# Flamingo-style gated cross attention with an RWKV feed-forward: a late weight load, its buffer, one split and the prologue put in another order

## What is computed

```python
x = x + tanh(g_xattn) * attention(layernorm(x), ctx, ctx, mask, q_w, q_b, k_w, k_b, v_w, v_b, o_w, o_b)
x = x + tanh(g_ffn) * ffn(layernorm(x), W_r, W_k, W_v, mu_r, mu_k)
# attention: Q, K, V = x@q_w.T+q_b, ctx@k_w.T+k_b, ctx@v_w.T+v_b, in 16 heads
#            softmax(Q K^T / sqrt(32), masked) V, then @ o_w.T + o_b
# ffn: x_prev is x moved down by one row; xr, xk = mu*x + (1-mu)*x_prev
#      sigmoid(xr @ W_r.T) * (relu(xk @ W_k.T)**2 @ W_v.T)
```

## Time and profile before

| | us |
|---|---|
| median of 3 runs | 1153.17 |
| lowest and highest | 1152.59, 1156.04 |
| the profiled execution | 1153.75 |
| its span, first to last instruction | 1151.9 |
| PE busy | 1118.8 (97%) |
| DVE busy | 888.4 (77%) |
| ACT busy | 686.3 (60%) |
| POOL busy | 367.6 (32%) |

### The profile page before, as it was taken

How to read it: one execution, slowest core, us unless ns; L and a number is a source line. 1 busy time by engine, 2 the same in 40 slices (tenths; PEclk the granted TensorE clock), 3 DMA queues, 4 the chain that set the end, 5 groups by cost and what they waited for, 6 DMA issues and landing times.

```text
span 1151.9 us, 21580 instructions
## 1 busy us (share of the span) xinstructions
PE 1118.8 (97%) x7216; PEld 895.2 (78%) x7216; DVE 888.4 (77%) x1964; ACT 686.3 (60%) x1527; POOL 367.6 (32%) x595
## 2 busy tenths in 40 slices
PE   5999999999999999999999999979999999999998
PEld 4677777777778778777877777757888888888886
DVE  7878877888788878887888788867677776776764
ACT  4767776777677767776777677753333323332232
POOL 0153153045045026116214302663442334323331
PEclk9999999999999999999999999989999999999999
DMA  8675575764775676567567557702311132111300
GB/s 284 199 199 146 166 212 153 193 193 132 199 203 131 192 207 171 139 196 214 149 168 211 141 144 229 222 12 74 99 55 56 55 95 71 55 55 62 103 20 37
DMA packets 95709, 162.48 MB, mean 141 GB/s; under 512 B 13296, under 2 KB 22640, under 8 KB 95472
## 3 DMA queue, kind: packets, MB, share of 16 engines
q1 hardware_dynamic: 84912, 143.37, 44.0%
q10 hardware_dynamic: 10688, 17.73, 5.4%
HBM read 109.91 MB, written 49.57 MB: 138 GB/s over the span
## 4 chain that ended last, share of the span: by engine, by line
PE 87%; DMA 3%; issue 2%; DVE 2%; POOL 1%; ACT 1%; SPq 0%; DVEq 0%; ACTq 0%; POOLq 0%
PE bank L550 26%; PE bank L624 18%; PE bank L586 14%; PE bank L615 10%; PE bank L636 9%; PE bank L594 8%; PE bank L749 1%; DMA w_raw<-wvvT 1%; ACT kact_hi L985 1%; PE bank L738 1%; DMA rden_dram<-ctx_sb 0%; DVE xh L1238 0%; POOL w2r_lo L1429 0%; DVE kact L1276 0%; DMA qk_dram<-q_hi 0%
## 5 line engine op out<-in xcount | busy, mean ns | idle before, releaser
L904 ACT ACTIVATE probs<-neg_s,negmax 128x512 f32<-128x512 f32 x512 | 368.1, 720 | 65.0 <-DVE negmax L1079 62.7
L1079 DVE CUSTOM_DVE_ANT_0 neg_s<-bank,mask_big 128x512 f32<-128x512 f32 x512 | 344.0, 679 | 9.7 <-DVE mask_big L1139 1.0
L624 PE MATMUL bank<-ident,probs 128*128 128x128 f32 x2048 | 307.6, 273 | 3.0 <-DVE pT L1085 2.9
L624 PEld LDWEIGHTS bank<-ident,probs 128*128 128x128 f32 x2048 | 248.1, 140 | 51.1 <-issue 6.1
L1085 DVE COPY pT<-bank 128x512 f32<-128x512 f32 x254 | 175.0, 689 | 110.2 <-PE bank L624 109.1
L615 PE MATMUL bank<-k_stack,q_stack 96*128 96x512 f32 x512 | 242.1, 473 | 0.2 <-DMA q_stack<-qk_dram 0.2
L911 ACT COPY pT<-bank 128x512 f32<-128x512 f32 x258 | 149.8, 580 | 127.6 <-PE bank L624 127.0
L636 PE MATMUL bank<-pT,v_sb 128*32 128x512 f32 x1024 | 116.5, 595 | 0.6
L983 ACT ACTIVATE relu<-bank 128x512 f32<-128x512 f32 x32 | 19.2, 599 | 145.3 <-PE bank L550 143.3
L615 PEld LDWEIGHTS bank<-k_stack,q_stack 96*128 96x128 f32 x512 | 97.3, 190 | 1.6 <-DMA q_stack<-qk_dram 0.5
L904 ACT ACTIVATION_READ_ACCUMULATOR probs<-neg_s,negmax 128x1 f32 x512 | 97.1, 190 | 0.0
(11 more groups left out here) (158 smaller groups left out, 2165.3 us busy)
## 6 DMA issues: line engine op xcount, KB each, us to landing
k_stack<-qk_dram SPq DMA_DIRECT2D x93, 256.0 KB, 5.4
q_stack<-qk_dram SPq DMA_DIRECT2D x93, 256.0 KB, 6.2
cT_raw<-ctxT SPq DMA_DIRECT2D x8, 1024.0 KB, 7.6
rden_bc<-rden_dram SPq DMA_DIRECT2D x128, 64.0 KB, 6.2
ctx_dram<-ctx_sb SPq DMA_DIRECT2D x32, 256.0 KB, 2.2
c_raw<-ctx_dram SPq DMA_DIRECT2D x16, 512.0 KB, 5.0
x_in<-x SPq DMA_DIRECT2D x16, 512.0 KB, 5.8
qk_dram<-k_hi SPq DMA_DIRECT2D x31, 256.0 KB, 2.7
```

The source lines that it names most:

```text
L624: mm = nc.tensor.transpose(pt_bank[i % 2][:, a * P:(a + 1) * P], probs[:, i % P_RING, a * P:(a + 1) * P], ident[:])
L904: nc.scalar.activation(probs[:, i % P_RING, :], neg_s[:, i % SM_RING, :], ACT.Exp, bias=negmax[:, k:k + 1], scale=-1.0, accum_out=den[:, g ...
L1079: nc.vector.tensor_tensor_reduce(neg_s[:, i % SM_RING, :], s_bank[tile_no(b, c, i) % S_BANKS][:], mask_big[:, q, :], 1.0, 3e38, ALU.add, A ...
```

## The change

The diff changes four things:

- **The fourth late weight** (wvv) is loaded into `w2_raw[0]`, the buffer of the first, as soon as that one is split, from SP's group 1 of the last batch (before: into `w2_raw[1]` after the second's split, from group 2). x1 moves over `w2_raw[1]`.
- **POOL's order at the passage:** the third split (wr) goes behind the inverse root and the second unit's context; the second bias goes ahead of the root.
- **Prologue:** `ident` is the first transfer after x; on PE the second keys go ahead of the first queries, and V0 takes the low part of the weight last; on ACT the first keys go ahead of the query weight's rounding; on DVE the mask goes ahead of Q0 and the scaling of the bias row (`gate_bias`) to step (1, 1); ACT starts the query copies after the high part of Q0.
- **Batch 1's x:** two of the four statistics go into the prologue, the others to steps (0, 9) and (0, 13); ACT's store, first two loads and spread go to steps (1, 0) to (1, 3), and the last load from (2, 0) to (1, 15).

```diff
@@ -78,8 +78,8 @@
     if nb == 1:
-        return {(0, 0, 0): ("xT", 0), (0, 0, 2): ("xT", 1), (0, 0, 12): ("store", 0), (0, 1, 0): ("spread", 0),
-                (0, 1, 14): ("xT", 2), (0, 2, 0): ("xT", 3)}
+        return {(0, 1, 0): ("store", 0), (0, 1, 1): ("xT", 0), (0, 1, 2): ("xT", 1), (0, 1, 3): ("spread", 0),
+                (0, 1, 14): ("xT", 2), (0, 1, 15): ("xT", 3)}
     return {(first, 3, 0): ("rows", 0), (first, 3, 2): ("rows", 1), (first, 3, 10): ("rows", 2),
@@ -87,7 +87,7 @@
-    return ((0, 0, 1), (0, 0, 3), (0, 0, 5), (0, 0, 7)) if nb == 1 else (
+    return (None, None, (0, 0, 9), (0, 0, 13)) if nb == 1 else (
         (nb - 2, 3, 7), (nb - 2, 3, 9), (nb - 1, 0, 3), (nb - 1, 0, 5))
@@ -206,7 +206,7 @@
-        x1 = [w2_raw[0][:, h * UM:(h + 1) * UM, :] for h in range(2)]
+        x1 = [w2_raw[1][:, h * UM:(h + 1) * UM, :] for h in range(2)]
         xh = sb(stage2, "xh", [P, UM, D])
@@ -351,9 +351,9 @@
                 load_x(t)
+            sp.dma_start(ident[:], ident_d).then_inc(ident_ld, 16)
             load_w(1, wk)
             load_ctx(0)
-            sp.dma_start(ident[:], ident_d).then_inc(ident_ld, 16)
             for t, a in ((bq_col, bq), (bk_col, bk)):
@@ -428,8 +428,8 @@
                 if n == 3:
-                    sp.wait_ge(w2_lo_done[1], 1)
-                sp.dma_start(w2_raw[n % 2][:], W2[n].rearrange("(a p) e -> p a e", p=P)).then_inc(w2_ld[n % 2], 16)
+                    sp.wait_ge(w2_lo_done[0], 1)
+                sp.dma_start(w2_raw[n % 3][:], W2[n].rearrange("(a p) e -> p a e", p=P)).then_inc(w2_ld[n % 3], 16)
@@ -481,8 +481,8 @@
                         load_turned(0, 1)
+                        load_w2(3)
                     if c == 2 and not more:
-                        load_w2(3)
                         load_w2r()
@@ -648,6 +648,18 @@
+            def first_values(keys):
+
+                for act_part, w in ((act_hi, w1_hi), (act_lo, w1_hi), (act_hi, w1_lo)):
+                    if w is w1_lo:
+                        pe.wait_ge(w_lo_done, 3)
+                    for a in range(CH):
+                        mm = nc.tensor.matmul(first_v_bank[:, keys * UNIT:(keys + 1) * UNIT],
+                                              act_part[1][:, a, keys * P:(keys + 1) * P], w[2][:, a, 0:UNIT],
+                                              start=act_part is act_hi and w is w1_hi and a == 0,
+                                              stop=w is w1_lo and a == CH - 1)
+                return mm
+
             def chunk_rounded(a):
@@ -663,26 +675,27 @@
+            product(1, 1, second_bank[1], w1_hi, act_hi, start=True)
+            product(1, 1, second_bank[1], w1_lo, act_hi)
+            product(1, 1, second_bank[1], w1_hi, act_lo, stop=True).then_inc(second_mm[1], 1)
+
             pe.wait_ge(w_hi_done, 2)
             pe.wait_ge(side_hi, hi_no(None, ("T", TT - 1)) + 1)
             product(0, 0, q_first, w1_hi, act_hi, start=True)
             pe.wait_ge(side_done, done(side_no(None, ("T", TT - 1))))
             product(0, 0, q_first, w1_hi, act_lo)
-            product(1, 1, second_bank[1], w1_hi, act_hi, start=True)
-            product(1, 1, second_bank[1], w1_lo, act_hi)
+            pe.wait_ge(side_done, done(side_no(None, ("K", 0))))
+            product(0, 1, second_bank[0], w1_hi, act_hi, start=True)
             pe.wait_ge(w_lo_done, 2)
             product(0, 0, q_first, w1_lo, act_hi, stop=True).then_inc(side_mm, 1)
-            product(1, 1, second_bank[1], w1_hi, act_lo, stop=True).then_inc(second_mm[1], 1)
-
-            pe.wait_ge(side_done, done(side_no(None, ("K", 0))))
-            product(0, 1, second_bank[0], w1_hi, act_hi, start=True)
             product(0, 1, second_bank[0], w1_hi, act_lo)
             product(0, 1, second_bank[0], w1_lo, act_hi, stop=True).then_inc(second_mm[0], 1)
-            pe.wait_ge(w_lo_done, 3)
-            side(None, "V", 0, 0, 2)
+
+            pe.wait_ge(w_hi_done, 3)
+            first_values(0)
             for i in range(AHEAD_S):
                 scores(0, 0, i)
-            side(None, "V", 0, 1, 2)
+            first_values(1).then_inc(side_mm, 1)
             scores(0, 0, AHEAD_S)
@@ -850,6 +863,8 @@
                 for band, source in enumerate((qk_hi, qk_hi, qk_lo)):
+                    if j == 0 and band == 2:
+                        act.wait_ge(side_done, done(side_no(None, ("Q", 0))))
                     act.dma_start(stack[0][0][HD * band:HD * (band + 1), j, :].bitcast(F32),
@@ -915,12 +930,12 @@
                     nc.scalar.mul(bq_neg[:], bq_col[:], -SCALE).then_inc(consts, 1)
+                if (kind, n) == ("Q", 0):
                     split_w(0)
-                if (kind, n) == ("Q", 0):
                     split_w(2)
                     act.wait_ge(consts, 1)
                 side(None, kind, n)
-            act.wait_ge(side_done, done(side_no(None, ("Q", 0))))
+            act.wait_ge(side_hi, hi_no(None, ("Q", 0)) + 1)
             for j in range(2):
@@ -1132,19 +1147,23 @@
             split_w(0)
+            dve.wait_ge(mask_ld, 16)
+            nc.vector.tensor_scalar(mask_big[:], mask_u8, MASKED, None, ALU.mult).then_inc(mask_done, 1)
             dve.wait_ge(consts, 1)
             side(None, "Q", 0)
             split_w(2)
-            dve.wait_ge(mask_ld, 16)
-            nc.vector.tensor_scalar(mask_big[:], mask_u8, MASKED, None, ALU.mult).then_inc(mask_done, 1)
+            for t in range(2):
+                row_stats(1, t)
             dve.wait_ge(mask_done, 1)
             mask_and_min(0, 0, 0)
             mask_and_min(0, 0, 1)
+            mask_and_min(0, 0, 2)
             dve.wait_ge(bv_ld, 16)
             side(None, "V", 0)
-            mask_and_min(0, 0, 2)
-            dve.wait_ge(consts, 2)
-            nc.vector.tensor_scalar(tgbo[:], tgbo[:], tg[:, 0:1], None, ALU.mult).then_inc(consts, 1)
+
+            def gate_bias():
+                dve.wait_ge(consts, 2)
+                nc.vector.tensor_scalar(tgbo[:], tgbo[:], tg[:, 0:1], None, ALU.mult).then_inc(consts, 1)
@@ -1160,6 +1179,8 @@
                         tile_step(b, c, i)
+                        if (b, c, i) == (0, 1, 1):
+                            gate_bias()
                         if i == TILES - 2:
@@ -1187,7 +1208,7 @@
                     if m == 0:
-                        dve.wait_ge(w2_lo_done[0], 1)
+                        dve.wait_ge(w2_lo_done[1], 1)
                         dve.wait_ge(xb_done, 1)
@@ -1416,11 +1437,11 @@
             def split_w2(n):
-                raw = w2r_raw if n == 2 else w2_raw[n % 2]
+                raw = w2r_raw if n == 2 else w2_raw[n % 3]
                 if n == 2:
                     pool.wait_ge(w2r_ld, 16)
                 else:
-                    pool.wait_ge(w2_ld[n % 2], 16 * (n // 2 + 1))
+                    pool.wait_ge(w2_ld[n % 3], 16 * (n // 3 + 1))
                 pool.wait_ge(side_mm, mm_no(B - 1, (("Q", 3), ("K", 3), ("V", 3), ("V", 3))[n]) + 1)
@@ -1450,10 +1471,10 @@
             split_w2(3)
-            split_w2(2)
+            first_bias(1)
             inverse_root2(0, 0)
             first_context(1)
-            first_bias(1)
+            split_w2(2)
             for b in range(B):
```

## The result

| | median (us) | lowest to highest | runs |
|---|---|---|---|
| before | 1154.86 | 1152.59 to 1156.04 | 7 |
| after | 1149.56 | 1146.58 to 1151.96 | 7 |

After over before is 0.9955, with a 95% interval of 0.9941 to 0.9969: 5.3 us or 0.45% faster. The forecast was 1144.2 with a range of 1141.5 to 1148.0. So the sign was right and the size was not: 9.0 us were forecast, and the median lies 1.6 above the range. Of the 5.4 us between 1149.56 and 1144.2, 1.7 lie in the kernel before, whose median over seven runs is 1154.86 and not the 1153.17 of the three that the forecast started from; the other 3.7 are the change. Note the spread too. The profiled execution of after, 1146.58 us for a span of 1144.7, is the fastest of its seven.

What follows compares the result with a forecast made beforehand. PE, busy 97% of the span, was taken as the bound, with stage 1 waits at the start and the passage. Passage 6.7 plus prologue 2.3 made 9.0 us off 1153.17, so 1144.2, range 1141.5 to 1148.0.

Steps and rivals of the forecast that it cites:

- The sum for the passage: Passage to stage 2: 6.95 us of DVE's wait and 1.3 of clock gained, 1.5 lost to POOL; 6.7 us net.
- The meeting of DVE and POOL: After the root, POOL's third split beside DVE's difference and mix: costs 1.5 us, bounds 0 and 3.
- Transfers around 719 to 743: Last batch: the fourth weight's megabyte ahead of SP's stores and stacks costs 0, with a loss of up to 3 us possible.
- The prologue up to group 1: Start of batch 0: first mask 0.8 us sooner, second keys' memory chain faster, q_stack landing at 47.7; 2.3 us gained.
- Batch 1's x costed at nothing: Later statistics, spread and loads of batch 1's x cost 0, with the steps of group 1 as cover.
- The clock: At the passage, a wait of 1.1 us keeps PE's clock, gaining 1.3 us; losing it would give 1145.5.
- The prologue gives nothing: Rival: q_stack lands where it did and only the passage's 6.7 us remains, 1146.5 us; chance 0.14.
- My list of what would be wrong: Signs against: PE waits for last-batch stacks or batch 0 group 2 cT/xT parts; POOL waits for x_in or fourth weight beyond 749.8.

Runs made afterwards that it cites:

- the run with the split ahead: The kernel with after's edits but the old x chain, with POOL's third split put ahead of the root again: 1148.29 us against its base's 1146.51.
- the passage alone: The kernel before with only the passage's edits (fourth weight's earlier load and buffer, POOL's order, x1): 1148.09 us, ratio 0.9943.
- the kernel with a mended chain: After with batch 1's statistics at steps 1 and 3, store at 12, two x loads at 13 and 14 of group 0, spread at (1, 0): 1144.95, again 1144.88 us.
- the old chain: After with batch 1's whole x chain (statistics, store, spread, loads) back at its steps of the kernel before: 1146.51 us, ratio 0.9933.
- the prologue alone: The kernel before with after's prologue edits and new x chain, without the passage's edits: 1154.95 us, ratio 1.0005.

## Why the prediction was right and wrong

**The sum for the passage: right.** 6.7 forecast, 6.6 measured alone. By its steps in the profile of after: the root starts at 749.75 (749.8 forecast), DVE's wait of 6.95 is gone, the clock at 763 to 767 is 1.00 instead of 0.61, the difference is 7.77 sooner (8.25 forecast). The forecast of 1.1 us of wait ahead of the transposes was too much (0.36), but the 1.12 for ACT's copies of the turned rows behind them was not foreseen; about the same. The first was too much because the forecast moved xh as it was: the first xh took 1.35 before, beside POOL's c_hi, and takes 0.71 now, where most of them take 0.53.

**The meeting of DVE and POOL: right in kind, half too big.** The difference took 2.13 beside w2r_lo, 1.22 alone, so 0.91; no piece of the mix was held. 0.91 against the 1.5 taken, and 8.25 was 0.48 too much: that the two errors cancel to 0.1 is luck. The mix escaped because the split ended at 766.0 and it began at 766.11. POOL paid as well, 6.03 for four pieces instead of 4.97, and all of it in the last piece, 2.27 where the others took 1.28. The difference began at 762.71 and the last piece at 763.7: first DVE waited for the piece in progress, then the last piece for the difference. The exclusive lock of the Trainium skill (SBUF — State Buffer, Who interferes with whom) agrees with both numbers. The prediction's sentence on instructions with one SBUF input leaves out that the page excepts VectorE's two-port modes; xh has one such tensor and was held, as said above. The rule speaks against the move, and the run with the split ahead says the move is still worth 1.8.

**Transfers around 719 to 743: right.** No wait of PE for stacks in the last batch; the 0 taken held.

**The prologue up to group 1: right in sign, a little small.** q_stack landed at 47.09 (47.7 forecast), PE's first scores of group 1 moved from 50.05 to 47.13: 2.9 gained in this pair of executions, 2.3 forecast. A pair can mislead here: with the prologue of before, group 0's context product stood at 54.94 in the profile of before and at 56.70 in that of the passage alone. Which terms: the second keys' store took 2.0 to 2.1 and not 2.7, since I took the whole run's median for a transfer that now has the engines nearly to itself; k_hi came 1.26 sooner, as forecast; but the first mask came only 0.26 sooner, not 0.8, as V0 now waits 1.15 for the low part of wv, which itself came 0.70 later (28.05 against 27.35), with the mask's preparation ahead of it on DVE. I had `ident` help K0 only. Put back alone it costs 2.3.

**Batch 1's x costed at nothing: the step that failed.** I wrote that POOL waits for those loads and that PE needs the products in the middle of group 2, and took group 1 as cover. The last consumer was not the first to suffer. The load issue at step (1, 14) stands on ACT's queue between exponentials, and it waits for POOL. It had not been moved; what moved is POOL, which began 9.0 us later (68.50 against 59.47), 5.3 of them because the spread went out later. The rest is what I did not ask, what else is in flight when the spread goes out: 4.4 us at 54.9, 8.2 at 60.2. The last load, which was moved ahead to (1, 15), went out at 77.21 behind the held exponential; no run moves it alone. So a term put at 0 cost a stop of 2.75 us in the profiled execution. In the median it took the whole forecast gain of the prologue and 1 us more: after stands at 1149.0 to 1149.6, the passage alone at 1148.1, and the kernel with a mended chain at 1144.9.

**The clock: right in one place, missed in the other.** I argued that stops of up to 1.1 us keep it, and in after they did. I listed the clock as a risk in the passage only. With a new stop of 2.75 us in group 1, seven of 15 executions clearly lost some of it, and with that stop taken away by the old chain none of five did. That they lost it behind this stop was seen in the profile of the prologue alone, and only inferred for after.

**Rivals.** "The prologue gives nothing" (1146.5, 0.14) is the nearest to what happened, by a mechanism that it didn't name. My list of what would be wrong had waits for xT parts in group 2: that stayed away in after and appeared as soon as the chain was moved. With the chain mended the kernel stands at 1144.9, near the 1144.2 of the forecast; but it is another kernel, its gain is 9.5 to 10.2 us from a slower start, and `ident` alone is worth 2.3 in it, most of which I had not counted.

Open: why a stop of 2.6 to 3.0 us loses the clock in some executions and not in others, and how much of the spread of after comes from the prologue instead, where ACT's start on the key weight varies by 2.3 us.

## What to carry to other kernels

A step that is moved off a busy stretch must be followed to everyone who stands behind its waits: a DMA issue on an engine's queue is a wait on that engine, and the work behind it pays, long before the data's user does. Check a transfer's new place against what is in flight there: the landing time belongs to the moment, not to the transfer. And look at the spread with the median: where a profiled execution is the fastest of its kind and carries a new stop, compare the granted clock of the others before trusting the profile's price for that stop.

## What the runs showed of the hardware

- The granted clock behind a stop of PE, by the profiles (lowest windows of 4 us, in order, around and behind the stop): 1.00 behind 2.65, 2.65, 2.75 and 2.98 us, but 0.87 and 0.70 behind 2.57. Behind 3.47 it was 0.74 and 0.83, behind 3.92 it was 0.84 and 0.73, behind 4.82 it was 0.91 and 0.67, behind 5.83 it was 0.75, 0.50 and 0.89. Two stops of 1.15 and 1.59 with 0.7 us of work between them were followed by 0.70, 0.50 and 0.95; single ones of 1.74 and 1.98 by 1.00.
- A transfer's time to landing changed with its moment: 512 KB took 4.2 to 4.4 us ahead of SP's stack loads and 5.8 to 9.2 behind them; issued at 60.2 it landed at 68.4, issued at 62.9 it landed at 68.7. A store of 256 KB took 2.0 us without two x loads of 256 KB beside it and 3.3 to 3.7 with them.
- VectorE and GpSimd held each other up by whole instructions: a difference of 128x1024 took 2.13 us instead of 1.22, and the one piece of the split that met it 2.27 instead of 1.28.
- A load of 256 KB on POOL's queue, behind the stacks, was used 9.2 us after its issue (79.63 to 88.88). On ACT's queue a load of that size was used 6.4 us after its issue in after (77.21 to 83.62) and 7.4 in the run with the spread at step 5 (77.54 to 84.91); a pair near 49 us took 3.2. How much of the 9.2 is POOL's queue and how much the moment stays open.
